# Layer 1's gate scores on VectorE instead of TensorE in a fused graph and mixture-of-experts kernel

## The reference, cut to what matters

```
x = x + L0_gnn(layernorm(x));  x = x + L0_ffn(layernorm(x))
x = x + L1_gnn(layernorm(x));  x = x + L1_ffn(layernorm(x))

def _L1_ffn_ref(x, ...):                 # x is normalised, (1, 3125, 256)
    gates = softmax(x @ gW + gb)         # gW (256, 4), gb (4,): E = 4 experts
    topv, topi = top_k(gates, 2); topw = softmax(topv)
    return shared_mlp(x) + sum over the two chosen experts of topw * expert(x)
```

## Time and profile before

| | us |
|---|---|
| median of three runs | 1177.13 (1174.05 to 1177.28) |
| the profiled execution, its whole time | 1176.47 |
| its span, first to last instruction | 1174.9 |
| PE busy in the span | 1132.1 (96%) |
| DVE busy | 566.1 (48%) |
| ACT busy | 361.1 (31%) |
| dense and early part of this stage, tiles 0 to 9 | 853.7 to 947.9 |
| tiles 10 to 24 one after the other | 948.8 to 1038.4 |
| in 948 to 1039: PE, DVE, ACT busy | 90.2, 41.6, 8.9 of 91.0 |
| heads and the last group | 1038.4 to 1050.2 |
| last stage | 1050.6 to the end |

### The profile page before, as it was taken

The page is one execution under the profiler, slowest core; times in us unless marked ns, Lnnn a source line. Parts: engine busy times, 40 slices in busy tenths (PEclk is TensorE's granted clock), DMA queues, the critical chain, the costliest instruction groups (busy, mean ns, idle before and its releaser), DMA issues. The chain is left out here.

```text
span 1174.9 us, 22055 instructions
## 1 busy us (share of the span) xinstructions
PE 1132.1 (96%) x8024; PEld 852.8 (73%) x8024; DVE 566.1 (48%) x1540; ACT 361.1 (31%) x697; POOL 167.9 (14%) x158
## 2 busy tenths in 40 slices
PE   5989999999999997999999899999999999999998
PEld 3667777776668885888888777555566678866675
DVE  8878888834437678211111463000044355248654
ACT  5764444522210102333333333100122201034333
POOL 3300000000000546444444300000000000001000
PEclk9989999999999999999999899999999999999999
DMA  6710000037632346466674621120066445126101
GB/s 192 215 44 14 25 25 13 26 114 186 159 110 85 128 140 187 74 119 147 117 154 71 134 90 45 58 75 32 20 157 188 135 131 165 55 87 196 45 22 43
DMA packets 134553, 118.19 MB, mean 101 GB/s; under 512 B 23061, under 2 KB 122700, under 8 KB 134470
## 3 DMA queue, kind: packets, MB, share of 16 engines
q1 hardware_dynamic: 104022, 78.25, 23.4%
q0 software_dynamic: 12272, 18.37, 8.2%
q10 hardware_dynamic: 18176, 20.45, 5.1%
HBM read 67.34 MB, written 49.29 MB: 99 GB/s over the span
## 5 line engine op out<-in xcount | busy, mean ns | idle before, releaser
L1372 PE MATMUL b_pa<-adj,l_parts 128*128 (+2 forms) x980 | 141.7, 296 | 0.3 <-ACT adj L1303 0.3
L1372 PEld LDWEIGHTS b_pa<-adj,l_parts 128*128 128x128 f16 x980 | 91.2, 97 | 29.4 <-issue 0.4
L2748 PE MATMUL l_sum<-l_parts,ring 128*128 128x256 f32 x448 | 101.4, 379 | 1.5 <-ACT ring L2845 1.5
L1613 DVE SCALAR_TENSOR_TENSOR l_parts<-dense,scale,l_parts 128x256 f16<-128x256 f32 x48 | 23.2, 483 | 158.9 <-ACT l_parts L1604 158.8
L2943 POOL DMA_INDIRECT x<-ring,l_row_i x54 | 84.2, 1558 | 106.1 <-DVE ring L2890 70.7
L1580 PE MATMUL dense<-room,ring 128*128 128x512 f32 x200 | 93.9, 593 | 0.1
L2748 PEld LDWEIGHTS l_sum<-l_parts,ring 128*128 128x128 f32 x448 | 83.0, 190 | 11.9 <-issue 1.7
L2299 PE MATMUL l_sum<-l_parts,adj 128*128 128x256 f16 x735 | 82.9, 273 | 1.2 <-DVE rows L2027 1.2
L2299 PE MATMUL l1b_sum<-l_parts,adj 128*128 128x256 f16 x735 | 82.9, 273 | 0.9 <-DVE rows L2027 0.9
L2299 PEld LDWEIGHTS l_sum<-l_parts,adj 128*128 128x128 f16 x735 | 71.2, 98 | 10.7 <-issue 2.7
L2299 PEld LDWEIGHTS l1b_sum<-l_parts,adj 128*128 128x128 f16 x735 | 71.4, 98 | 10.4 <-issue 2.4
(11 more groups left out here) (473 smaller groups left out, 1863.1 us busy)
## 6 DMA issues: line engine op xcount, KB each, us to landing
ring<-sums_and_zt SPq DMA_DIRECT2D x50, 256.0 KB, 3.4
l_expert_xr<-slots_in SPq DMA_DIRECT2D x28, 257.0 KB, 2.8
l_parts<-in_L_ffn_W SPq DMA_DIRECT2D x12, 512.0 KB, 4.7
pre<-room ACTq DMA_DIRECT2D x34, 128.0 KB, 1.8
sums_and_zt<-ring SPq DMA_DIRECT2D x10, 320.0 KB, 2.3
ring<-inv SPq DMA_DIRECT2D x50, 64.0 KB, 4.0
sums_and_zt<-room ACTq DMA_DIRECT2D x5, 640.0 KB, 3.4
adj<-xt SPq DMA_DIRECT2D x5, 640.0 KB, 4.4
```

Of the source, the lines that this page charges most:

```text
L1372: ins = nc.tensor.matmul(pa[f][:, 0:size], parts[:, k, a, f * P:(f + 1) * P], adj[:, k, ds(r * BW, size)], start=k == 0 and a == 0, stop=k ...
L1613: return nc.vector.scalar_tensor_tensor(parts[:, k, 1, :], bank[:, 0:D], scale, parts[:, k, 0, :], ALU.mult, ALU.subtract)
L2748: ins = nc.tensor.matmul(to[t], h[:, n, t * P:(t + 1) * P], w2[:, u, n, :], start=i == 0, stop=i == HB - 1)
```

## The change

For `routing` nothing changes. For layer 1, PE no longer runs `score` and `back` (nor `rank`, which did nothing there), and ACT no longer runs `take_flat`. The gate weights come as rows: SP's DMA at k = 5 broadcasts the 256 x 4 matrix to all partitions (512 KB in place of 4 KB), and DVE turns it once into [4, 256] on each partition (1024 elements read with a step of four words). `take_scores(c)` is now one `scalar_tensor_tensor` with a running sum (`accum_out`) for each tile and each expert, 256 elements wide: 100 in all, 16 for a group of four tiles. Each waits for the last but one before it, since two product buffers alternate. A wait and one addition of the bias follow. DVE's order becomes `finish_early`, `final.constants`, `take_scores(0)`, `take_scores(1)`, then for c from 2: `finish(c)`, `take_scores(c)`. SP loads over groups 0, 1 and 2 only when their scores are done. ACT's wait in `take_turned` on `multiplied` goes.

```diff
+            gate_in_rows = pr.sb("gate_in_rows", [P, D, E], F32)
+            gate_rows = pr.sb("gate_rows", [P, E, D], F32)
+            products = pr.sb("products", [P, 2, D], F32)
...
+                        sp.dma_start(gate_in_rows[:, :, :], gate_w.rearrange("(a d) e -> a d e", a=1).broadcast_to([P, D, E])).then_inc(s["gate_in"], 16)
...
             for c in (3, 4, 5):
                 if routing:
                     sp.wait_ge(s[f"scattered{AFTER[c]}"], 16 * 2 * SIZES[AFTER[c]])
+                else:
+                    sp.wait_ge(s["score_done"], E * STARTS[AFTER[c] + 1])
...
             def take_scores(c):
-                dve.wait_ge(s["scored"], c + 1)
-                nc.vector.tensor_tensor(g["scores"][:, tiles_in(c), 0:E], score_at(c),
-                                        bg[:, :].unsqueeze(1).broadcast_to([P, SIZES[c], E]), ALU.add).then_inc(s["score_done"], 1)
+                dve.wait_ge(s["norm_done"], STARTS[c + 1])
+                dve.wait_ge(s["gate_padded"], 1)
+                for n in range(SIZES[c]):
+                    t = STARTS[c] + n
+                    for e in range(E):
+                        if E * t + e >= 2:
+                            dve.wait_ge(s["score_done"], E * t + e - 1)
+                        nc.vector.scalar_tensor_tensor(products[:, e % 2, :], normed(c)[:, n, :], 1.0, gate_rows[:, e, :], ALU.mult, ALU.mult,
+                                                       accum_out=g["scores"][:, t, e:e + 1]).then_inc(s["score_done"], 1)
+                dve.wait_ge(s["score_done"], E * STARTS[c + 1])
+                ch.mark(nc.vector.tensor_tensor(g["scores"][:, tiles_in(c), 0:E], g["scores"][:, tiles_in(c), 0:E],
+                                                bg[:, :].unsqueeze(1).broadcast_to([P, SIZES[c], E]), ALU.add))
...
-            nc.vector.memset(strips_of_wg[:, :, E:STRIP], 0.0)
-            nc.vector.tensor_copy(strips_of_wg[:, :, 0:E], wg[:, :, :]).then_inc(s["gate_padded"], 1)
+            if routing:
...
+            else:
+                nc.vector.tensor_copy(gate_rows[:, :, :], gate_in_rows[:, :, :].rearrange("p d e -> p e d")).then_inc(s["gate_padded"], 1)
...
                 for c in range(FINISHES):
+                    if c >= 2:
+                        finish(c)
                     take_scores(c)
-                    if c + 2 < FINISHES:
-                        finish(c + 2)
...
+                elif routing:
+                    act.wait_ge(s["multiplied"], c)
                 else:
-                    act.wait_ge(s["multiplied"], c)
-                    if not routing:
-                        act.wait_ge(s["xt_out"], 16 * c)
+                    act.wait_ge(s["xt_out"], 16 * c)
...
             def take_flat(c):
+                if not routing:
+                    return
...
-                    {"turn": turn, "score": score, "back": back, "rank": rank}[what](c)
+                    if routing or what == "turn":
+                        {"turn": turn, "score": score, "back": back, "rank": rank}[what](c)
```

More of the change, by code:

```diff
@@ L1829, in second_conv @@
             weights = expert_weights(parts, pr.sb("expert_w1", [P, KD, H0], F32), pr.sb("expert_b1", [P, 2, HB], F32))
-        wg = pr.sb("gate_w", [P, KD, E], F32)
-        strips_of_wg = held[1][:, 0:KD * STRIP].rearrange("p (k e) -> p k e", k=KD)
+        if routing:
+            wg = pr.sb("gate_w", [P, KD, E], F32)
+            strips_of_wg = held[1][:, 0:KD * STRIP].rearrange("p (k e) -> p k e", k=KD)
+        else:
+            gate_in_rows = pr.sb("gate_in_rows", [P, D, E], F32)
+            gate_rows = pr.sb("gate_rows", [P, E, D], F32)
+            products = pr.sb("products", [P, 2, D], F32)
         bg = pr.sb("gate_b", [P, E], F32)
@@ L1909, in load_vectors @@
                 elif k == 5:
-                    sp.dma_start(wg[:, :, :], gate_w.rearrange("(k p) e -> p k e", p=P)).then_inc(s["gate_in"], 16)
+                    if routing:
+                        sp.dma_start(wg[:, :, :], gate_w.rearrange("(k p) e -> p k e", p=P)).then_inc(s["gate_in"], 16)
+                    else:
+                        sp.dma_start(gate_in_rows[:, :, :], gate_w.rearrange("(a d) e -> a d e", a=1).broadcast_to([P, D, E])).then_inc(s["gate_in"], 16)
                     sp.dma_start(bg[:, :], gate_b.rearrange("(a e) -> a e", a=1).broadcast_to([P, E])).then_inc(s["gate_in"], 16)
@@ L2140, in _ @@
             dve.wait_ge(s["pre_out1"], 16 * uses(1))
-            nc.vector.memset(strips_of_wg[:, :, E:STRIP], 0.0)
-            nc.vector.tensor_copy(strips_of_wg[:, :, 0:E], wg[:, :, :]).then_inc(s["gate_padded"], 1)
+            if routing:
+                nc.vector.memset(strips_of_wg[:, :, E:STRIP], 0.0)
+                nc.vector.tensor_copy(strips_of_wg[:, :, 0:E], wg[:, :, :]).then_inc(s["gate_padded"], 1)
+            else:
+                nc.vector.tensor_copy(gate_rows[:, :, :], gate_in_rows[:, :, :].rearrange("p d e -> p e d")).then_inc(s["gate_padded"], 1)
             if routing:
```

## The result

The changed kernel takes 1179.65 us (median of 7 runs), the kernel before 1175.82 beside it: a ratio of 1.0033, interval 1.0020 to 1.0046, so 2.4 to 5.4 us slower.

A forecast was written before the change was run, and what follows sets the result against it. DVE's in-order queue was taken to bound PE through its normalisations: the last at 1057.0 plus a 5.6 us tail gives 1062.6 against 1050.24, so +12.4 on 1176.5, predicted 1189 us; range 1182 to 1206.

The forecast's parts named there:

- What bounds the stage, and the deciding step: Tiles 10 to 24: PE's turns wait for DVE's normalisations; two score groups before group 2 cost 11.7 us at turn(2).
- What goes: PE's path: seven scores at 0.67 us and seven backs at 0.12 go, 5.5 us in all.
- The copy: DVE before tile 10: strided weights copy takes 1.1 us, delaying PE by 1.0, bounds 0.5 to 2.1.
- The price of a product: DVE's scores: product 0.42 plus sum read 0.09, taken as 0.50 us; 8.2 us for a group of four tiles.
- N2: End of DVE's normalisation of group 2, which turn(2) waits for; forecast at 996.0, before the change 981.77.
- N1: End of DVE's normalisation of group 1, which turn(1) waits for; forecast at 972.6, 1.0 us later than before.
- N6: End of DVE's normalisation of group 6, the last; forecast at 1057.0, before the change 1043.79.
- The clock: PE behind turn(2): half clock after the wait loses up to 3.2 us, covered by DVE; another 1 us if not.
- Rival 2: DVE's products run at half rate, 0.77 us each; kernel near 1215 us; chance 0.1.
- Rival 1: DVE's read of the sum is not overlapped, product 0.60 to 0.66 us; kernel 1198 to 1204; chance 0.2.
- Rival 3: DVE's products cheap at 0.42 and copy fast at 0.5 us; +5 to +6, kernel 1182; chance 0.1.
- Rival 4: PE stays the bound at turn(2): 5.5 us go, 1.0 is added, kernel 1172, faster; chance 0.03.

The follow-up runs named there:

- e5: Changed kernel with DVE's order alone undone, group 2 finished before scores 0 and 1; ratio 0.9993 to the kernel before.
- e11: Changed kernel with one more plain product of the same shape for every two, into an unread buffer; ratio 1.0095 to the kernel before.
- e9: Kernel before with SP's load of group 3's rows held back until group 1's store landed; run once, stage 103.0 us.
- e10: Changed kernel with DVE's order undone, weights' copy among dense products, score products laid tile by tile into DVE's waits; ratio 0.9964 to the kernel before.
- e1: Changed kernel with the product's scalar read from SBUF in place of the immediate 1.0; run once, 1185.0 us.
- e2: Changed kernel with its products but without the running sum; sixteen products in 5.45 us, whole time not given.
- e8: Changed kernel without its products, scores being the bias alone; ratio 0.9969 to the kernel before.

## Why the prediction was right or wrong, point by point

- **What bounds the stage, and the deciding step.** Right: PE's turn waits for a normalisation that stands behind scores in DVE's queue; one wait, at `turn(2)`, by L2055, as named. e5 takes it away by the order alone, e11 makes it 11.88 by the price alone.
- **What goes.** Right: 0.79 us for each score and back; five of them give the 4.0 of the table, the tail 1.5.
- **The copy.** Right: 1.09 long, 1.01 from start to start, against 1.1; tile 10 waits 0.9 us longer, against 1.0. That the 1.1 fitted so well is in part luck: no row had such a step, and the bounds were 0.5 and 2.1. The DMA of 512 KB cost PE nothing, as assumed: between 863 and the end of the early products PE's timeline shows no wait.
- **The price of a product. This step failed.** The term "0.42 + 0.09 = 0.50" (it adds up to 0.51) measured 0.346. The row had a pointer scalar, the new instruction hasn't; the read was priced by another engine. The floor of the range, 0.42, came from the same row, so even the cheap rival lay above what happened. 32 products ahead of N2 were 4.9 us too dear, and the wait was 6.7, not 11.7. Three smaller misses nearly cancelled: N1 came 1.1 us early, the landing took 0.6 longer, PE reached `turn(2)` 0.4 early. e11 pays the forecast's price and gets 11.9 and +11.1 us.
- **What follows from the price.** At 5.8 us for a group DVE catches up behind `turn(2)`: a cycle is 10.1 and the landing, against PE's 16.9. No wait at `turn(3)` to `turn(5)` where I had 1.3 and a balance, and N6 at 1047.5 comes 4.7 us behind the last tile, not 7.7 (5.5 in e11).
- **N1 and the landing.** N1 came 21.7 us behind the start of tile 10, forecast 22.8, for the reason shown by e9; the landing of group 2's store took 4.5, forecast 3.95. `turn(1)` didn't wait, so PE did gain by the first score and back.
- **The clock.** Half right. The half clock came and cost 2.8 us (forecast: up to 3.2). That DVE would cover it failed with the price: PE was the bound behind `turn(2)`, and it counted in full. In e11 the half clock came too, and DVE did cover it.
- **Rival 2, half rate.** Wrong: 0.346 us for two f32 sources with a running sum, 0.335 without. The Trainium skill's sentence on that (Vector Engine (DVE) Microarchitecture Reference, Points that are easy to get wrong) doesn't hold here: the addition of 1024 elements, also of two f32 sources, takes 1.27 us from start to start, so 256 elements at half that rate would take about 0.6.
- **The read as an instruction of its own** is as the Trainium skill says (VectorE: DVE Perf Modes, Two Vector instructions with no wait between them): DVE_READ_ACCUMULATOR has a row behind each product. What it costs, 0.01 us, no row before could tell.
- **Rival 1** (read not overlapped) is wrong by the same rows. **Rival 3** was the nearest, and right in its shape: some of the scores came back once PE was the bound. Its price of a product was still too high, its copy of 0.5 us too low. **Rival 4** fell as argued: even at 0.346, 32 products are 11 us, and 4.7 were to be had.

## What to carry to other kernels

When work moves to an engine that is idle half of the time, don't count its free time; write down when each thing that the bound engine waits for is finished, in the order of the queue. Most of the gain was there once the new work stood in waits that DVE had anyway (e10), and lost where it stood in front of a normalisation (after) or behind the last one (e5).

Price a new instruction by a row with the same kinds of operands, and where there is none let the range go below the nearest row too: an operand that the new one doesn't have may be what made the row dear. And when a wait on the bound engine appears or goes, look at the clock in the next stretch as well: there it cost 2.8 and about 2 us more than the wait itself.

## What the runs showed of the hardware that I had not expected

- A DVE product of 256 f32 elements costs 0.346 us with a constant and 0.407 with a scalar from SBUF.
- Its running sum costs 0.01 us, though the read is shown as 0.08 long.
- A memset of 0.10 us between two such products costs 0.008: the product behind it is shown 0.05 shorter. Something in the distance of two products (0.346 for 256 elements) is filled by the memset; what, I did not find.
- An f32 copy of 1024 elements takes 1.01 us with a source step of four words and 0.61 without.
- PE's clock was at half after it stood still for 3.4 us between the two stages (e5), and not after 1.2 us at the same place (before, e10). The length of the wait alone doesn't decide: in front of tile 10 PE stood still for 1.92 and 2.03 us in e1 and e2, and its clock fell to 0.50 within tile 10; in e8 it stood still for 2.02 us and the clock stayed at 1.00. What tells these apart, the runs do not show.
- A store of 512 KB landed in 5.1 us with a load of 512 KB issued 1.8 us before it, and in 4.0 with that load held back (before, e9).
